# A second mixture of experts whose norm, gate and row scatter run inside the attention program

## The reference

```python
x = x + _attention(_layernorm(x, ln1_g, ln1_b), Wq, bq, Wk, bk, Wv, bv, Wp, bp)   # 16 heads, causal
x = x + _token_moe(_layernorm(x, ln2_g, ln2_b), gate_W, gate_b, exp_W1, exp_b1, exp_W2, exp_b2)
...
logits = flat @ gate_W + gate_b                    # 8 experts
top_v, top_i = jax.lax.top_k(logits, 2)
w = jax.nn.softmax(top_v, axis=-1)
for e in range(8):                                 # hidden size 1024, width 256
    mid = gelu(flat @ exp_W1[e] + exp_b1[e])
    out = out + w_full[:, e:e+1] * (mid @ exp_W2[e] + exp_b2[e])
```

## Time and profile before

| | us |
|---|---|
| median of 3 runs | 2826.07 (2823.96 to 2826.38) |
| the profiled execution | 2821.3 |
| its span, first to last instruction | 2819.5 |
| PE busy | 2510.2 (89%) |
| DVE busy | 1492.1 (53%) |
| ACT busy | 1328.4 (47%) |
| POOL busy | 445.9 (16%) |
| mean granted clock of PE | 0.952 of full |

### The profile page before, as it was taken

How to read it: one execution, slowest core, us unless ns; L and a number is a source line. 1 busy time by engine, 2 the same in 40 slices (tenths; PEclk the granted TensorE clock), 3 DMA queues, 4 the chain that set the end, 5 groups by cost and what they waited for, 6 DMA issues and landing times. The chain is left out here.

```text
span 2819.5 us, 47227 instructions
## 1 busy us (share of the span) xinstructions
PE 2510.2 (89%) x15793; PEld 1440.7 (51%) x15794; DVE 1492.1 (53%) x4176; ACT 1328.4 (47%) x2833; POOL 445.9 (16%) x687
## 2 busy tenths in 40 slices
PE   6999999899979889998799999999998993599991
PEld 3555544444434456675466544444445653377661
DVE  2555877788544500023555688877746654222224
ACT  2655466667744422111355557666665551122220
POOL 4233221101100000000123312212023001400004
PEclk8999999999989999999799999999999995699996
DMA  7545533233000022113644543242223318201103
GB/s 222 162 142 144 139 98 94 53 80 79 1 1 0 1 95 95 63 49 120 196 128 141 144 98 94 53 116 71 66 86 98 101 44 292 96 30 33 33 30 95
DMA packets 153825, 259.89 MB, mean 92 GB/s; under 512 B 22713, under 2 KB 96705, under 8 KB 149441
## 3 DMA queue, kind: packets, MB, share of 16 engines
q1 hardware_dynamic: 150544, 248.81, 30.9%
q0 software_dynamic: 3072, 8.39, 0.9%
HBM read 180.71 MB, written 81.53 MB: 93 GB/s over the span
## 5 line engine op out<-in xcount | busy, mean ns | idle before, releaser
L1449 ACT ACTIVATE second_p<-psum 128x512 f32<-128x512 f32 (+3 forms) x1024 | 461.1, 522 | 234.7 <-PE psum L1291 231.2
L1449 ACT ACTIVATE first_p<-psum 128x512 f32<-128x512 f32 (+3 forms) x768 | 366.6, 548 | 164.2 <-PE psum L1291 160.8
L1541 DVE TENSOR_REDUCE second_max_parts<-psum 128x1 f32<-128x512 f32 x512 | 322.6, 683 | 67.6 <-PE psum L1268 65.5
L1541 DVE TENSOR_REDUCE first_max_parts<-psum 128x1 f32<-128x512 f32 x512 | 322.6, 683 | 63.3 <-PE psum L1268 61.0
L1537 DVE CUSTOM_DVE_ANT_0 second_masked<-psum,mask_qk 128x384 f32<-128x384 f32 (+3 forms) x512 | 229.4, 488 | 180.9 <-PE psum L1268 160.5
L1303 PE MATMUL psum<-second_p,second_v_aug 128*32 128x512 f32 (+3 forms) x2048 | 232.8, 527 | 6.0 <-ACT second_p L1449 4.8
L1268 PE MATMUL psum<-second_k,second_q 64*128 64x512 f32 (+3 forms) x1024 | 199.4, 386 | 28.3 <-DMA second_k<-a_k_parts 14.3
L1281 PE MATMUL psum<-second_q,second_k 64*128 64x512 f32 (+3 forms) x1024 | 222.1, 430 | 2.5 <-ACT second_shift_T L1460 0.7
L1291 PE MATMUL psum<-second_shift_T,choose 64*128 64x512 f32 (+3 forms) x1024 | 194.9, 376 | 0.0
L1281 PEld LDWEIGHTS psum<-second_q,second_k 64*128 64x128 f32 x1024 | 96.6, 184 | 182.1 <-ACT second_p L1449 76.5
L1303 PE MATMUL psum<-first_p,first_v_aug 128*32 128x512 f32 (+3 forms) x1536 | 184.9, 554 | 1.1 <-ACT first_p L1449 0.7
(11 more groups left out here) (337 smaller groups left out, 3867.5 us busy)
## 6 DMA issues: line engine op xcount, KB each, us to landing
first_k<-c_k_parts SPq DMA_DIRECT2D x64, 256.0 KB
second_q<-a_q_parts SPq DMA_DIRECT2D x128, 128.0 KB, 2.9
second_k<-a_k_parts SPq DMA_DIRECT2D x128, 128.0 KB, 2.9
second_k<-c_k_parts SPq DMA_DIRECT2D x64, 256.0 KB, 4.5
first_q<-a_q_parts SPq DMA_DIRECT2D x64, 128.0 KB
first_k<-a_k_parts SPq DMA_DIRECT2D x64, 128.0 KB
c_k_parts<-first_held SPq DMA_DIRECT2D x16, 512.0 KB, 3.1
first_q<-c_q_parts SPq DMA_DIRECT2D x64, 128.0 KB
```

The source lines that it names most:

```text
L1449: evacuated(act.activation(probs[tile % 2][:, 2 * h + p, q0:SEQ], bank[:, q0:SEQ], ACT.Exp, scale=scale), event)
L1541: evacuated(v.reduce_max(max_parts[n % 2][:, h, p, qt, k0 // BANK:k0 // BANK + 1], bank[:, 0:width], axis=AX_X), event)
```

## The change

The stages gate_in and stage_gate are gone. Their work is now pieces of "second": for each batch b of a2, behind its output projection, come `gate_stats`, `gate_aggregate`, `gate_root`, `gate_scale`, `gate_add` (the layer norm), two `gate_turn` (transposes), `gate_logits`, `gate_top`, `gate_rank`, `gate_place` and `gate_send` (8 indirect DMAs of POOL). For batches 0 to 2 they are spread over the groups that follow; for batch 3 they stand behind the last group. rows_dram now has a fixed region of 2048 rows for each expert, so that a row's place needs no count of the tiles of other experts; `row_of` gives the first row of each of the 39 tiles, and `result_at` the row of each result in the packed list of results. The fill of the regions is 8 copies of x (2 MB each), issued by SP at the end of "first".

The weights `up` are loaded at groups 39 to 46 into an SBUF area that the context tiles, the held parts and most attention weights used before; `down` goes into the area of the q, k and probability tiles as they come free at the end. block_in is now in DRAM: SP stores x_tok there in place of POOL's copy, and loads it back (`residual`) in the experts' program, where POOL adds it. The experts' second bias is added to each result there (`down_bias`) and no longer on x_tok. SP reads `row_of` into a register for each tile, DVE `expert_of`.

```diff
+def gate_pieces(slot):
+    first = [("gate_add", slot, 0)] + [("gate_turn", slot, k) for k in range(DK)] + [("gate_logits", slot, 0)]
+    return first, [("gate_top", slot, 0)], [("gate_rank", slot, 0)], [("gate_place", slot, 0), ("gate_send", slot, 0)]
...
-COST = {"rest": 3000, "rms_turn": 450, "oturn": 450, "xturn": 450, "oproj": 1750, "split": 1750, "value": 1750}
+COST = {"rest": 3000, "rms_turn": 450, "gate_turn": 450, "gate_logits": 900, "oturn": 450, "xturn": 450, "oproj": 1750, "split": 1750, "value": 1750}
...
+    if layer.gated:
+        pieces.insert(3, ("gate_stats", slot, 0))
+        pieces += [("gate_stats", slot, 1), ("gate_aggregate", slot, 0), ("gate_root", slot, 0), ("gate_scale", slot, 0)]
...
+                def keep_rows(slot):
+                    sp.wait_ge(applied, QT * (norm_at[before_x(slot)] + 1))
+                    sp.dma_start(slots[slot].copy_to[slot % BATCH].rearrange("(q p) d -> p q d", p=P), x_of(slot)).then_inc(copied, 16)
...
+                    elif event[0] == "up":
+                        load_up(event[1])
+                    elif event[0] == "down" and gate:
+                        load_down()
...
                         fetch_weights(later_loads, later_in)
+                        if gate:
+                            fetch_weights(gate_loads, gate_in)
...
+                def gate_send(slot):
+                    b = slot % BATCH
+                    pool.wait_ge(gate_placed, b + 1)
+                    pool.wait_ge(gate_rows, QT * (b + 1))
+                    if b == 0:
+                        pool.wait_ge(gate["rows_filled"], 16 * E)
+                    for t in range(QT):
+                        for x in range(2):
+                            at = place[:, x, b * QT + t:b * QT + t + 1]
+                            pool.indirect_dma_start(gate["rows_dram"][:, :], bass.IndirectOffsetOnAxis(ap=at, axis=0),
+                                                    rows[:, t, :], None).then_inc(gate_sent, 16)
+                    if b == BATCH - 1:
+                        pool.wait_ge(gate_sent, 16 * 2 * NT)
...
+                def gate_scale(slot):
+                    b = slot % BATCH
+                    v.wait_ge(gate_in, 16 * len(gate_loads))
+                    for k in range(DK):
+                        wait_full(v, ("gate_turn", slot - 1, k) if b else ("xturn", len(slots) - 1, k))
+                    wait_for(v, gate_sent, 16 * 2 * QT * b)
...
-                    sp.dma_start(rows[r][:, :], rows_dram[bass.ds(t * P, P), :]).then_inc(rows_in[r], 16)
+                    sp.dma_start(rows[r][:, :], rows_dram[bass.ds(rows_of(sp, t), P), :]).then_inc(rows_in[r], 16)
...
+                sp.dma_start(down_bias[:, :, :].rearrange("p e d -> p (e d)"),
+                             a["L1_ffn_exp_b2"].rearrange("e d -> (e d)").partition_broadcast(P)).then_inc(down_bias_in, 16)
+                for b in range(BATCH):
+                    sp.dma_start(residual[:, b * QT:(b + 1) * QT, :], block_in[b].rearrange("(q p) d -> p q d", p=P)
+                                 ).then_inc(residual_in, 16)
                 for_steps(sp, body)
...
-                        v.tensor_copy(result[r][:, :], c.psum[:, DOWN_BANK + r, 0:D]).then_inc(y_read, 1)
+                        e = weights_of(v, t)
+                        v.tensor_tensor(result[r][:, :], c.psum[:, DOWN_BANK + r, 0:D],
+                                        down_bias[:, bass.ds(e, 1), :].rearrange("p o d -> p (o d)"), ALU.add).then_inc(y_read, 1)
...
+            turned, best, ranked, placed = gate_pieces(slot)
+            if b < BATCH - 1:
+                pieces[first + 1] = pieces.get(first + 1, []) + output_pieces(a2, slot)
+                pieces[first + 2] = [REST] + turned
+                pieces[first + 3] = best + [REST] + ranked + [REST] + placed
+            else:
+                pieces[first] = output_pieces(a2, slot) + turned + best + ranked + placed
+        for e in range(EXPERTS):
+            contexts[2 * NG + BATCH + 3 + e] = [("up", e, 0)]
```

536 lines of the change are left out of this document (324 added, 212 removed).

## The result

The changed kernel takes 2813.96 us (median of 5 runs, 2807.25 to 2815.59) against 2826.38 for the kernel before in the same set of runs: a ratio of 0.9945, 95% interval 0.993 to 0.9961. It is 12 us faster where 51 were forecast, and outside the range. The profiled execution took 2807.25 us with a span of 2805.4: 14.05 us less than the one of before.

A forecast was written before the change was run, and what follows sets the result against it. Between attention and the experts a chain with no full engine was taken as the bound, in attention PE. A tail gain of 75.4 us less additions of 24.6 gave 50.8 faster: 2775 us for the median, range 2757 to 2792.

The forecast's parts named there:

- The tail: From attention's last x_tok to the experts' first matmul: only batch 3 is left, 35.3 us against 110.7, a gain of 75.4.
- item 8: DVE's small steps beside the last 8 scatters lengthen them: 1 us taken, near 2 at most.
- Item 1: Gate transposes, logits and ranks of three batches added to PE inside a2: 8.5 us, bounds 5 and 10.
- Item 2: Gate blocks on DVE inside a2 delay the maxima PE needs: 3 us, bounds 0 and 27.
- rival C: DVE's blocks in a2 become stalls of PE: 13.5 us in place of 3, giving 2785.5; chance 12%.
- Item 3: POOL's scatters of a batch inside a2, 10.2 us, cost nothing, as POOL is mostly idle there.
- Item 4: Start of "second": four more loads ahead of the context delay PE by 2.1 us.
- Item 5: Start of the experts' program: bias and residual loads queue ahead of the second tile's rows, 9 us, bounds 3 and 12.
- Item 6: Register loads on SP and DVE: 1 us ahead of the first rows, bounds 0.3 and 2; nothing in the loop.
- E: Register loads lengthen each of the experts' 39 steps; from 6.2 us a load the kernel is slower; chance 3%.
- F: A load of up blocks SP in a2 and keys come late; 50 us gone would be no change; chance 2%.

The follow-up runs named there:

- sets A, D and E: Follow-up sets of runs, each beside the kernel before: single edits, then all blocks cut, then the changed kernel and scatters in pairs; every version showed a pause.
- e3: Changed kernel with the second bias loaded behind the second tile's rows and the residual behind the rows of tiles 2 to 5: 1.0 of before.
- e11: Changed kernel with gate_add earlier, gate loads, bias and residual later, plus logits in four pieces and scale and add in halves: 2785.72 us, 0.9856 of before.
- e5: The changed kernel again, unchanged: 2813.73 us, 0.9951 of before.
- e9: Changed kernel with gate_add earlier, gate loads, bias and residual later, plus logits in four pieces: 0.9882 of before.
- e10: Changed kernel with gate_add earlier, gate loads, bias and residual later, plus scale and add as halves of two tiles: 0.9859 of before.
- set E: Last set of runs, with the pause; in it the changed kernel, unchanged, took 2837.21 us, 1.0034 of before.
- B and C: Two sets of runs without the pause; in them the changed kernel, unchanged, took 2813.73 us (0.9951 of before) and 2814.92 us (0.9954).

## Why the prediction was wrong

By its own steps, for the two profiled executions:

- **The tail** (75.4 less 2 for items 6 and 8): 73.4. Right in the sum, and by luck to the tenth, for the parts cancel: from the last scatter's end to PE are 11.5 us where 7.9 and 1 were taken, the chain ahead of the first scatter took 15.7 where the parts gave 16.9, and the scatters 10.0 where 10.4 and 1 for item 8 were taken. Item 8 is near 0 (1.30 us each beside DVE, 1.28 before). That the longer border is the register load is argued, not shown.
- **Items 1 and 2** (8.5 and 3): 38.5. This is the step that failed, 27.0 of the 36.8 us missed. Item 1 has about its size: some 7 of the 29.1 us that PE was busy longer aren't the clock, and 8.5 were forecast. Item 2 said that DVE "can lose one block's length without PE's noticing", and its upper bound was the sum of all blocks, 27. PE does notice: 1.9 and 2.5 us of a block reach it, 9.4 us in all over before, where 3 were taken. And behind these waits, and once behind the narrow logits, stand 44 us at half clock, an estimated 22 us, a cost that isn't in the list and for which the sum of the blocks is no upper bound; rival C had the stalls, priced at 13.5, but not the slow clock behind them. The rows of before had both levels of the clock, one in attention and one in the tail, and the price of the logits was even taken at half clock and then halved; that the added pieces would themselves bring the level down was not asked.
- **Item 3**: nothing, in the first profile. In sets A, D and E the same scatters come with up to 10 us at group 40 and 44 each, which the prediction had nowhere and whose cause stays open.
- **Item 4**: 5.4 in place of 2.1; the loads themselves 1.4 to 2.2, the rest open.
- **Item 5**: the second tile waits 9.6 where it waited 0.6, 9.0 more as forecast, and 9.5 came back in e3. This is as the Trainium skill (DMA: Bandwidth & Descriptors, Queues, rings and completion order) has it: descriptors of one queue are consumed in ring order on each DMA engine.
- **The rest**, 6.5 us: 0.8 at the start of "second", 1.3 in small shifts of its groups, 2.4 because the last output projection stands in a slow stretch, 2.0 behind the second tile's rows, 1.6 of them in the experts' first products, which now run at half clock. With 27.0 and 3.3: 36.8.
- **Item 6**: no row stood behind the 1 us for the register load ahead of the first rows, and no run measured it alone. The loop's step stayed at 7.98 us, so in the loop the loads cost nothing. Neither `down` nor batch 2's scatters were waited for (they end 6.5 us ahead of `gate_scale`): E and F did not happen.

## What to carry to other kernels

Work moved under a full PE is not priced by its own length: ask of each piece whether its order on another engine can make PE wait, because here the slow stretch behind a wait of 1.4 to 2.5 us could cost several times as much, and put the producer a pause ahead of the consumer and cut blocks on the engine that PE follows. When one such place is mended the next block takes its turn, so read the granted clock window by window after each edit. And small transfers that open a program go ahead of the large ones that nothing needs yet.

## What the runs showed of the hardware

- Behind waits of 1.3 to 2.5 us in a PE that is otherwise full stood anything from nothing (1.3 us in the kernel before, 1.7 in e11) to 17 us at 0.5 (1.4 us in group 46 of e5, 1.9 in batch 1 of the changed kernel). The length isn't set by the wait alone: one of 2.5 was followed by 3.4 us in batch 0 and by 17 in batch 1 of the same run (e9). Useless transposes in place of a wait of 1.9 kept 1.0 until the logits. A wait of 1.3 ahead of an output projection was followed by 3.4 us at 0.5 in e10, and by none in the kernel before; there the window with the wait, and the next:

```profile
2236.00:2240.00 4.00, 2.72 (x18) 1.98 (x16) 0.82 (x7) 1.88 (x4) 0.09 (x1) 1.00 0.70 207
2240.00:2244.00 4.00, 3.90 (x42) 2.53 (x42) 2.81 (x10) 1.66 (x5) 0.00 (x0) 1.00 0.13 38
```

- A block of 16 narrow matmuls (128 x 8, 1.9 us) was followed by the same fall, for 6.8 us, without idle time of PE right ahead of it; cut into two blocks of eight with other work between, it was not (e10 against e11, groups 38 and 42).
- Eight scatters of 128 rows beside loads of keys and queries came with stops of PE, DVE and ACT together, of 2.4 to 4.6 us of PE, in three sets of runs and in two others not, with the same program (1.0034 of before in set E, 0.9951 and 0.9954 in B and C).
